# Message layer of a graph network by groups of four tiles, with a rearranged setup

## What is computed

```python
deg = segment_sum(ones, col)
dis = where(deg > 0, rsqrt(maximum(deg, 1.0)), 0.0)
x = layernorm(x + segment_sum(x[row] * (dis[row] * dis[col])[:, None], col))

s, v = x[:, :8], x[:, 8:].reshape(n, 8, 3)
w = (relu(edge_feat @ W1 + b1) @ W2 + b2).reshape(e, 4, 8, 8)
s_e, v_e = s[src], v[src]                      # gathered rows
sh0, sh1 = edge_sh[:, 0], edge_sh[:, 1:4]
m0 = ALPHA * (einsum('ei,eio->eo', s_e * sh0[:, None], w_000)
              + C110 * einsum('eim,em,eio->eo', v_e, sh1, w_110))
m1 = ALPHA * (einsum('ei,em,eio->eom', s_e, sh1, w_011)
              + einsum('eim,eio->eom', v_e * sh0[:, None, None], w_101))
# m0, m1 summed by destination, si_w0 and si_w1 applied to s and v, layer norm
```

## Time and profile before

| What | us |
|---|---|
| time, median of three runs (3348.32 to 3350.93) | 3349.41 |
| the profiled execution's own time | 3349.01 |
| its span | 3347.2 |
| TensorE busy | 2663.4 (80%) |
| VectorE busy | 2810.8 (84%) |
| ScalarE busy | 1171.6 (35%) |
| GpSimd busy | 2384.1 (71%) |
| setup, to the first counted one-hots | 0 to 94.25 |
| degree layer, to the first gather of the message layer | 94.25 to 1204.40 |
| message layer, to the last message | 1204.40 to 3329.62 |

### The profile page before, as it was taken

One profiled execution on the slowest core, in us unless ns is written; L12 is line 12 of the kernel. 1 busy time (PEld: TensorE's weight loads), 2 busy tenths in 40 slices (PEclk: granted clock), 3 DMA queues, 4 the chain that ended last, 5 costly groups with the idle time before them and its releaser, 6 DMA issues.

```text
span 3347.2 us, 48324 instructions
## 1 busy us (share of the span) xinstructions
PE 2663.4 (80%) x17534; PEld 1593.1 (48%) x17534; DVE 2810.8 (84%) x4461; ACT 1171.6 (35%) x1339; POOL 2384.1 (71%) x2475
## 2 busy tenths in 40 slices
PE   5699999999999977777777777777777777777776
PEld 4467777766676743333333433333333333333433
DVE  7877777777777739998998998989889898898987
ACT  2688788887878741111111111111111111111110
POOL 0677777777777747777777777777777777777774
PEclk7799999999999978888888888898888888888887
DMA  2200100000000121111111111111111111111112
GB/s 54 30 14 14 14 14 14 14 14 14 14 14 14 17 32 32 28 28 28 28 31 28 28 28 28 28 28 32 28 28 28 28 28 28 31 28 28 28 28 35
DMA packets 188500, 84.47 MB, mean 25 GB/s; under 512 B 131897, under 2 KB 174713, under 8 KB 188281
## 3 DMA queue, kind: packets, MB, share of 16 engines
q0 software_dynamic: 78336, 40.26, 8.0%
q1 hardware_dynamic: 109945, 41.21, 5.6%
HBM read 76.48 MB, written 4.81 MB: 24 GB/s over the span
## 4 chain that ended last, share of the span: by engine, by line
POOL 44%; issue 16%; DVE 1%; POOLq 0%; PE 0%; DMA 0%; ACT 0%; DVEq 0%; ACTq 0%
POOL xg L555 44%; DVE stage L1485 0%; PE ps L784 0%; POOLq L563 0%; POOLq L549 0%; POOLq L542 0%; PE ps L750 0%; DVE prod_all L1475 0%; DMA xg<-x_table,idx 0%; DVE prod_all L1469 0%; DVE oh L1163 0%; POOLq L142 0%; ACT stage L665 0%; DVE sumT_all L1183 0%; DVE z_sq L1245 0%
## 5 line engine op out<-in xcount | busy, mean ns | idle before, releaser
L555 POOL DMA_INDIRECT xg<-x_table,idx x1664 | 1571.9, 945 | 565.5 <-issue 531.5
L555 POOL DMA_INDIRECT xg<-scaled_x_table,idx x784 | 804.9, 1027 | 336.0 <-issue 233.6
L920 PE MATMUL ps<-w2t,hT 128*128 128x512 f32 x1664 | 950.3, 701 | 36.0 <-ACT hT L656 36.0
L605 ACT ACTIVATE room<-ps 128x1089 bf16<-128x1089 f32 x800 | 880.7, 1204 | 209.2 <-PE ps L797 208.9
L1485 DVE TENSOR_REDUCE stage<-prod_all 128x192 f32<-128x1536 f32 x416 | 725.7, 1745 | 3.2
L797 PE MATMUL ps<-prod_all,lane 128*128 128x363 bf16 x2640 | 562.5, 322 | 118.0 <-ACT room L605 63.1
L915 PE MATMUL ps<-b2p,ones_b 128*128 128x512 bf16 x832 | 308.4, 459 | 354.0 <-DVE prod_all L1475 354.0
L920 PEld LDWEIGHTS ps<-w2t,hT 128*128 128x128 f32 x1664 | 373.1, 229 | 419.5 <-issue 295.2
L656 ACT ACTIVATE hT<-ps,b 128x512 f32<-128x512 f32 x208 | 138.4, 666 | 1132.4 <-PE ps L908 1132.4
L1469 DVE TENSOR_TENSOR prod_all<-ps,stage 128x768 f32<-128x768 f32 x416 | 397.4, 955 | 92.0 <-ACT stage L665 55.9
L812 PE MATMUL ps<-stage,room 128*128 128x96 bf16 x7840 | 465.8, 207 | 0.0
(11 more groups left out here) (150 smaller groups left out, 1511.3 us busy)
## 6 DMA issues: line engine op xcount, KB each, us to landing
efT<-in_efT SPq DMA_DIRECT2D x104, 256.0 KB
xg<-x_table,idx POOLq DMA_INDIRECT x1664
xg<-scaled_x_table,idx POOLq DMA_INDIRECT x784
sh<-in_sh SPq DMA_DIRECT2D x104, 32.0 KB
idx<-in_src SPq DMA_DIRECT2D x104, 8.0 KB, 1.6
idx<-in_src SPq DMA_DIRECT2D x98, 4.0 KB
scaled_x_table<-room SPq DMA_DIRECT2D x2, 784.0 KB, 7.6
x_table<-x_sb SPq DMA_DIRECT2D x7, 224.0 KB, 4.5
```

Of the source, the lines that this page charges most:

```text
L555: pool.indirect_dma_start(rows[k][:, t, :], None, table, bass.IndirectOffsetOnAxis(ap=idx[k][:, tile:tile + 1], axis=0),).then_inc(s_g[lay ...
L605: act.activation(counts[u % 2][:, :, t * TWIN:(t + 1) * TWIN].rearrange("p (r h) w -> p r h w", r=RANGES), ps_ring[i % 2].rearrange("p r ( ...
L920: mm = pe.matmul(ps_bank[j % 2][v], hT[j // 2][:, t * P:(t + 1) * P], w2t[:].rearrange("p h c o i -> p (h c o i)"), start=False, stop=True)
```

## The change

In the **message layer** each gathered row group signals for itself: the gathers of group j of a chunk raise s_gg[k][j] instead of one semaphore per buffer. VectorE makes the dots of one group (96 elements instead of 384) just ahead of that group's products, with two operations per group, and ScalarE spreads one group at a time, two groups behind each hidden pair. A buffer is given back when the fourth group's dots and copies are made.

In the **setup** six things move. The 22 tile one-hots go ahead of the flag's wait. The eleven low one-hots become one wide one-hot of 16 x 128 elements and a copy of ten of its columns; step i reads a shifted part of it, now contiguous, as TensorE's weight. The key work goes ahead of the degree chain. The preparation of the weights (`prepare_weights`, its body unchanged but for the eps) goes to the end of the degree layer, ahead of the sums of unit U + 1. The scaled table is written so that a partition's 98 rows lie together (row 98 l + h instead of 128 h + l); and the source indices of all 49 gathered chunks are loaded in the setup (`load_sources`, the same loads that the counted tiles already had, 20 more of them) and turned into the new row numbers by two operations on VectorE and two on GpSimd, of 784 elements per partition each. The 98 index loads of the degree layer go.

```diff
+        efT_all = sb("efT_all", [P, 2, TPG * P])
+        efT = [efT_all[:, k] for k in range(2)]
+        idx0 = efT_all[:].rearrange("p k e -> p (k e)")[:, 0:CG * TPC].bitcast(I32)
...
+        idx0_block = oh_all[1][:].rearrange("p t w -> p (t w)")[:, 0:CG * TPC].bitcast(I32)
...
+        LX = NC + TWIN - 1
+        lox = ohlo[0:CHUNKS, 0:TPC * LX].rearrange("p (t j) -> p t j", j=LX)
...
+        s_own = sem("s_own")
+        s_remap = sem("s_remap")
...
+        s_gg = [[sem(f"s_gg{k}_{j}") for j in range(GPC)] for k in range(2)]
...
+            for n in range(PATTERNS):
+                a = n * CPP * TPC
+                load_sources(idx0[:, a:a + gathered_in(n)], n * PT, gathered_in(n), s_own)
...
-            def load_indices(layer, n):
+            def load_indices(n):
...
+                    for j in range(GPC):
+                        sp.wait_ge(s_gg[k][j], 16 * TPG * (n // 2))
+                sp.dma_start(idx[k][:], src_d[n]).then_inc(s_idx[k], 16)
...
-            y_v = y_d.rearrange("(h l) f -> l h f", l=P)
+                load_indices(n)
...
-            for n in range(2, CG):
-                load_indices(0, n)
...
-            def gather(layer, k, i, rows, table):
...
-                        pool.wait_ge(s_ft, 2 * (2 * i + k - 1))
-                        pool.wait_ge(s_scal, 2 * (2 * i + k - 1))
...
+            pool.wait_ge(s_remap, 2)
+            pool.tensor_scalar(idx0, idx0, NP, None, ALU.mult).then_inc(s_remap, 1)
+            pool.wait_ge(s_remap, 3)
+            pool.tensor_tensor(idx0, idx0, idx0_block, ALU.add).then_inc(s_remap, 1)
+
+            def gather_rows(to, table, at, landed):
+                pool.indirect_dma_start(to, None, table, bass.IndirectOffsetOnAxis(ap=at, axis=0)).then_inc(landed, 16)
+
...
+                    gather_rows(xg[n % 2][:, t, :], y_d, idx0[:, n * TPC + t:n * TPC + t + 1], s_g[n % 2])
+
+            def gather(k, i):
+                pool.wait_ge(s_idx[k], 16 * i + 16)
+                if not isinstance(i, int):
+                    pool.wait_ge(s_ft, 2 * GPC * (2 * i + k - 1))
+                    pool.wait_ge(s_scal, 2 * GPC * (2 * i + k - 1))
+                pool.sem_inc(s_begun[1], 1)
+                for t in range(TPC):
+                    tile = tile_of(t)
+                    gather_rows(xg[k][:, t, :], x1_d, idx[k][:, tile:tile + 1], s_gg[k][t // TPG])
...
-            def scalars(n):
+            def scalars(n, j):
                 k = n % 2
-                act.wait_ge(s_g[1][k], 16 * TPC * (n // 2 + 1))
-                if n >= 2:
+                cut = slice(TPG * j, TPG * (j + 1))
+                act.wait_ge(s_gg[k][j], 16 * TPG * (n // 2 + 1))
+                if n >= 2 and j == 0:
                     act.wait_ge(s_prod, 2 * GPC * (n - 1))
-                act.activation(feat[k][:, :, 0::2, :], xg[k][:, :, 0:MUL].unsqueeze(2).to_broadcast([P, TPC, 2, MUL]),
+                act.activation(feat[k][:, cut, 0::2, :], xg[k][:, cut, 0:MUL].unsqueeze(2).to_broadcast([P, TPG, 2, MUL]),
                                ACT.Copy).then_inc(s_scal, 1)
-                act.activation(vec[k][:].rearrange("p t m i -> p t i m"),
-                               xg[k][:, :, MUL:D].rearrange("p t (i m) -> p t i m", m=3), ACT.Copy).then_inc(s_scal, 1)
+                act.activation(vec[k][:, cut].rearrange("p t m i -> p t i m"),
+                               xg[k][:, cut, MUL:D].rearrange("p t (i m) -> p t i m", m=3), ACT.Copy).then_inc(s_scal, 1)
...
-                rectify(HPC * n)
-                scalars(n)
-                rectify(HPC * n + 1)
+                for m in range(HPC):
+                    rectify(HPC * n + m)
+                    for j in range(GPC // HPC * m, GPC // HPC * (m + 1)):
...
-                    a, b = ((ohhi_v, ohlo_v), (ohhi_w, ohlo_w))[i % 2]
-                    pe.wait_ge(s_ndoh, 3 * i + 10)
+                    a = (ohhi_v, ohhi_w)[i % 2]
+                    pe.wait_ge(s_ndoh, 2 * i + 11)
                     for t in range(TPC):
-                        mm = pe.matmul(ps_deg, b[0:CHUNKS, :, t], a[0:CHUNKS, :, t], start=False, stop=False)
+                        mm = pe.matmul(ps_deg, lox[:, t, TWIN - 1 - i:LX - i], a[0:CHUNKS, :, t], start=False, stop=False)
...
+            for i in range(4, CHUNKS // 4):
+                tile_one_hots(i)
             dve.wait_ge(s_span, 1)
             step(dve.tensor_reduce(near_f[:, 0:1], spans[:], AX_X, ALU.max))
             step(dve.tensor_scalar(near_f[:, 2:3], near_f[:, 0:1], 0.5, None, ALU.is_le))
             step(dve.tensor_tensor(near_f[:, 2:3], near_f[:, 2:3], near_f[:, 3:4], ALU.mult))
             dve.tensor_copy(near[:], near_f[:, 2:3]).then_inc(s_near, 1)
-            for i in range(4, CHUNKS // 4):
-                tile_one_hots(i)
...
+                dve.tensor_tensor(lox[:, :, TWIN - 1:LX], lo2[:, 0:TPC].unsqueeze(2).to_broadcast([CHUNKS, TPC, NC]),
+                                  lane_f[0:CHUNKS, 0:NC].unsqueeze(1).to_broadcast([CHUNKS, TPC, NC]),
+                                  ALU.is_equal).then_inc(s_ndoh, 1)
+                dve.wait_ge(s_ndoh, 8)
+                dve.tensor_copy(lox[:, :, 0:TWIN - 1], lox[:, :, NC:LX]).then_inc(s_ndoh, 1)
                 for i in range(TWIN):
                     if i >= 2:
                         dve.wait_ge(s_ndmm, i - 1)
                     cut = slice(TPC * i, TPC * (i + 1))
-                    ahi, alo = (halves(o, i % 2)[0:CHUNKS] for o in (ohhi, ohlo))
+                    ahi = halves(ohhi, i % 2)[0:CHUNKS]
                     dve.tensor_tensor(ahi[:, 0:NP, :], hi2[:, cut].unsqueeze(1).to_broadcast([CHUNKS, NP, TPC]),
                                       lane[0:CHUNKS, 0:NP, :], ALU.is_equal).then_inc(s_ndoh, 1)
-                    dve.tensor_tensor(alo, lo2[:, cut].unsqueeze(1).to_broadcast([CHUNKS, NC, TPC]),
-                                      lane[0:CHUNKS, 0:NC, :], ALU.is_equal).then_inc(s_ndoh, 1)
-                    dve.wait_ge(s_ndoh, 3 * i + 8)
+                    dve.wait_ge(s_ndoh, 2 * i + 10)
                     dve.tensor_tensor(ahi[:, 0:NP, :], ahi[:, 0:NP, :],
...
-            dve.wait_ge(s_degree, 1)
...
+            dve.wait_ge(s_own, 16 * IDX_LOADS)
+            dve.tensor_scalar(idx0_block, idx0, 7, None, ALU.logical_shift_right).then_inc(s_remap, 1)
+            dve.wait_ge(s_remap, 1)
+            dve.tensor_scalar(idx0, idx0, P - 1, None, ALU.bitwise_and).then_inc(s_remap, 1)
...
+            dve.wait_ge(s_degree, 1)
...
+            def prepare_weights():
+                dve.wait_ge(s_win, 128)
+                dve.wait_ge(s_pool_c, 3)
...
+                            dve.wait_ge(s_remap, 4)
...
+                        if t == 0 and u == U + 1:
+                            prepare_weights()
...
-            def features(n, k, landed, first):
-                dve.wait_ge(s_g[1][k], landed)
-                dve.wait_ge(s_shp, n + 1)
-                if not first:
-                    dve.wait_ge(s_prod, 2 * GPC * n)
-                    dve.wait_ge(s_ft, 2 * n)
-                dve.tensor_tensor(dots[:], xg[k][:, :, MUL:D].rearrange("p t (i m) -> p t i m", m=3),
-                                  ps_sh[k][:, :, 1:4].unsqueeze(2).to_broadcast([P, TPC, MUL, 3]),
+            def features(n, k, j, landed):
+                cut = slice(TPG * j, TPG * (j + 1))
+                made = 2 * GPC * n + 2 * j
+                dve.wait_ge(s_gg[k][j], landed)
+                dve.tensor_tensor(dots[:, cut], xg[k][:, cut, MUL:D].rearrange("p t (i m) -> p t i m", m=3),
+                                  ps_sh[k][:, cut, 1:4].unsqueeze(2).to_broadcast([P, TPG, MUL, 3]),
                                   ALU.mult).then_inc(s_ft, 1)
-                dve.wait_ge(s_ft, 2 * n + 1)
-                dve.tensor_reduce(feat[k][:, :, 1, :], dots[:], AX_X, ALU.add).then_inc(s_ft, 1)
+                dve.wait_ge(s_ft, made + 1)
+                dve.tensor_reduce(feat[k][:, cut, 1, :], dots[:, cut], AX_X, ALU.add).then_inc(s_ft, 1)
...
-                features(n, k, landed, first)
-                dve.wait_ge(s_ft, 2 * n + 2)
-                dve.wait_ge(s_scal, 2 * n + 2)
+                dve.wait_ge(s_shp, n + 1)
+                if not first:
+                    dve.wait_ge(s_prod, 2 * GPC * n)
+                    dve.wait_ge(s_ft, 2 * GPC * n)
                 if at >= 2:
                     dve.wait_ge(s_sum[1], n - 1)
                 if near_sums and at >= 1:
                     bases = load_bases(TPC * (n - 1))
                 for j in range(GPC):
+                    features(n, k, j, landed)
+                    dve.wait_ge(s_ft, 2 * GPC * n + 2 * j + 2)
+                    dve.wait_ge(s_scal, 2 * GPC * n + 2 * j + 2)
                     products(n, k, j, first and j < 2)
```

188 lines of the change are left out of this document (85 added, 103 removed).

## The result

The changed kernel takes 3307.01 us (median of four runs, 3303.95 to 3314.65) against 3349.11 of the kernel before: a ratio of 0.9877, with a 95% interval from 0.9864 to 0.9890. The profiled execution's span is 3304.0 against 3347.2: 43.2 less.

What follows compares the result with a forecast made beforehand. GpSimd's gathers in the message layer were taken as the bound (20.23 us per chunk), VectorE second with some 0.95 us slack. 3347.2 - 15.1 - 3 = 3329, plus 1.8 and 0.4: 3331 us; forecast 3324 to 3342, range 3316 to 3360.

Steps and rivals of the forecast that it cites:

- The setup, −15.1: Sum of the setup's terms before the message layer: -7.3 - 2 - 8.1 + 2 + 0.3 = -15.1 us.
- (a): Setup: the 22 tile one-hots move ahead and fill VectorE's 8.65 us wait for GpSimd's reduction; 7.3 us less.
- The rival that the one-hots don't fit beside the reduction: Setup: the one-hots don't fit there, or the table lands late; 7 us back, 3338 us; chance 1 in 10.
- (b): Setup, degree loop: one wide one-hot replaces eleven low ones; TensorE's step stays 2.75 us; about 2 us less.
- the rival of 8 us: Setup, degree loop: TensorE's step falls with contiguous weights; 8 us less, 3323 us; chance 2 in 10.
- (c): Setup, behind the degrees: key work moves ahead, weight preparation to the layer's end; about 8.1 us less.
- (d): Setup: scaled table written in long runs, gather indices turned to suit; VectorE waits for its landing; 2 us more.
- (e): Degree layer's end: weights prepared while VectorE waits for TensorE, 5.85 against 6.2 us idle; 0.3 us more (to 2).
- The message layer, −3: Message layer: taken between GpSimd leading (-11 + 4.5 = -6.5 us) and VectorE leading (+1 us).
- the end (11.3 less): Message layer's end: the last chunk's work no longer waits for its last row; 18.84 to about 7.7, 11 us less.
- the stall of 4.5: Message layer's start: GpSimd waits 4.5 us, once, at chunk 2 for chunk 0's buffer, freed after its fourth dots.
- VectorE as the bound, the chief rival: Message layer: larger gaps use up VectorE's slack, GpSimd waits every chunk; 38 us longer, 3372 us; chance 2 in 10.

## Why the prediction was wrong

*"The change leaves GpSimd's gathers of this layer as they are."* This is the step that failed. The prediction took 20.23 us per chunk as GpSimd's rate and the 531.5 us of idle time as issue in even steps of 0.32, while the steps are 0.30 and 14 pauses make up the rest. A mean over 1664 instructions hid a period of 112. The edit that looked like bookkeeping, one semaphore into four, took 23.5 us off the bound. 3307.0 and 23.5 are 3330.5, close to the forecast 3331, but only since the other misses, in the setup and at the start of the layer, cancel. That is luck. The single runs add up to the gain: 21.6 us for the signals alone, 8.1 for the setup alone and 11.3 for the layer's end are 41.0 of the 42.1.

*The setup, −15.1.* The sum came out at −15.7, its terms less well. (a) The degree part starts at 31.11 instead of 39.76, 8.7 earlier (7.3 forecast), but not because the one-hots fill a wait. GpSimd's first operation and its reduction, first before, then after with VectorE's one-hots:

```profile
10.51 0.55 POOL L494 IOTA lane_i<- 128x512 int32 x1 [10.08 <-issue]
28.05 0.39 POOL L525 PARTITION_ALL_REDUCE spans<-span  x1 [10.43 <-issue]
...
1.08 0.56 POOL L504 IOTA lane_i<- 128x512 int32 x1 [0.65 <-POOLq L1638]
18.20 0.39 POOL L535 PARTITION_ALL_REDUCE spans<-span  x1 [12.40 <-ACT stage L596]
...
18.86 10.57 DVE L1002 TENSOR_TENSOR room<-room,lane 128x704 bf16<-128x704 bf16 x22
```

The reduction is over at 18.59, before the first one-hot starts: there was no wait left to fill, and by these rows there would have been none in the old order either. GpSimd starts its work 9.4 us earlier, with the same instructions up to the reduction. All twelve traces with the new setup have it so (1.08 or 1.09), the four with the old one don't (10.4 to 10.5); what brings it about stays open. So (a) was right by luck. The rival that the one-hots don't fit beside the reduction was not put to the test, as they ran behind it, and the row that was held against it (19.53) doesn't bear on it, as the reduction itself stands at 28.05 there. (b) TensorE's 176 loads take 31.22 us, 0.177 each, against 0.172, at a granted clock of 0.50 in both loops, so contiguous weights make its step no shorter, and the rival of 8 us is wrong; the term came to 1.3 instead of 2. (c) came to 5.7 instead of 8.1. Its own sum is off by 0.5 (14.91 less 5.8 is 9.1, and with the 0.5 that sticks out 8.6), and the work moved ahead of the degrees took 7.2 us instead of 4.4: VectorE's key operations took longer beside GpSimd's two index operations, to which nothing was put. The rows stand at the end of this document; no run has them apart. (d) The table was no wait at all (2 forecast): the low part begins at 81.78, right behind the operation ahead of it.

*(e) The weights at the layer's end, 0.3.* They cost 2.4 us at the sum behind them, 1.2 at the addition after it. The 6.2 us of idle time were two waits, and the weights sat in the first, of 4.24, alone.

*Not forecast:* unit 2's wait for the first gathered chunk, 4.15 us. "The first gathers have the whole first unit" was said of GpSimd's index operations; but the unit now starts 15.7 earlier and the gathers only 12.2 earlier. Slow gathers are not what is new: three of the first are slow here (3.77, 2.63, 4.23), two were before (3.69, 4.23), and the first 16 took 27.6 us then and take 28.3 now.

*The message layer, −3.* VectorE's chunk (19.55) and the end (11.3 less) were right, and so was the stall of 4.5, where TensorE is at half clock. VectorE as the bound, the chief rival, didn't come: dependent gaps are 0.03 to 0.04, four waits or two. But it is now level with GpSimd, since GpSimd got faster by what was its slack.

## What to carry to other kernels

Before a rate is taken as fixed, look at its single steps: a mean with a wait that "issue" explains may hold a pause with a period, and a period that fits no loop of the program points at something countable, such as the signals. Where an engine issues thousands of gathers, give the landings more semaphores than buffers; here two more took 20 us off, with nothing else changed. When a term is freed at the front, ask of each later wait whether it was covered by time that is now gone. And when a wait is gone after a reordering, look at both of its ends before the reordering gets the credit: here it was the other engine that had come earlier.
